# The last normalisation of the node block moved from the node stage into the first two graph layers

## The chip, the cores and the metric

The kernel runs on one core of a Trainium2 chip. The metric is the device time of one execution in microseconds (us). The engines of the core are named as in the profile: PE (TensorE, matmuls), DVE (VectorE), ACT (ScalarE), POOL (GpSimd) and SP (SyncE, which here only issues DMAs). Each engine works through its own instruction stream in order; semaphores tie the streams together, and DMA queues move data between DRAM and the on-chip memory (SBUF). Matmul results land in PSUM.

## The reference

A node table `x` of 50000 rows by 128 goes through four graph blocks, each followed by a residual add and a layer normalisation over the 128 columns. There are 25000 edges, so most nodes receive no edge.

```python
x = _layernorm(x + _L0_gnn_ref(x, ...))   # attention over 4 heads, gelu, norm, + x
x = _layernorm(x + _L1_gnn_ref(x, ...))   # three graph layers of width 128
x = _layernorm(x + _L2_gnn_ref(x, ...))   # attention over 8 heads
x = _layernorm(x + _L3_gnn_ref(x, ...))   # attention over 4 heads, edge gate
```

For a node without an incoming edge the last block comes down to its bias, so its output row is

```python
out = _layernorm(x3 + L3_gnn_bias)        # x3: the row after the third block
```

The kernel computes this row for all nodes and later overwrites the rows of nodes that have edges.

## The kernel before

The program is a list of stages with a barrier of all engines between them (`all_meet`). Three of them matter here.

**The node stage** (lines 400 to 829) treats every node as if it had no edges. It takes the 50176 padded rows in 49 chunks of 1024 rows, a chunk lying on the 128 partitions with 8 rows each (`wide`). It is a software pipeline written out by hand: in iteration `t` every engine does one piece for each of several chunks at different depths, and the order of the statements is the order on the engine. Six normalisations, LNA to LNF, belong to one chunk. DVE takes the statistics of each (`stats`, four BATCH_NORM_STATS2 of 256 columns), then once per iteration computes the inverse roots of all six together in ten short dependent instructions on a 128x48 block (lines 722 to 775, ending in `scaled`), and ACT applies scale and shift (`apply`, line 596, eight ACTIVATE of 128x128). After `scaled`, DVE goes on with the pieces of the chunks, ACT starts its own row of pieces, and PE works between them. SP stores each finished tile. LNF is the last: at lines 801 to 810 DVE waits for `x3` of chunk t-7, adds `bias3` into `hf_b` and takes its statistics; ACT applies LNF to `hf_b` one iteration later (lines 686 to 689); SP stores it to `out` (line 457). The rows before LNF, `x3_b`, are stored to a DRAM table (`tables[4]`) as well (line 452). Beside all that POOL gathers rows of the edges' ends by indirect DMA and writes an index map. The stage has 58 iterations.

**The graph layers** (lines 1502 to 1669) are one stage per layer, three in all, over the edges' rows in 49 chunks of 512. In iteration `t`: SP loads `own` (the chunk's own rows) and stores `xw` of chunk t-4, in this order and in one in-order stream, each store waiting for ACT. POOL gathers the source rows `gs` by four indirect DMAs a chunk, up to six chunks ahead. PE transposes `gs` and `own` and multiplies chunk t-2 by the next weights. DVE adds the bias to `own` (line 1630, four instructions), runs the segment scan (line 1635) and adds both (line 1642, `u`). ACT applies relu (line 1593, `hT`) and scales the product (line 1601, `xw`). The third layer has in addition a residual, statistics, square root and normalisation of its own (lines 1608, 1615, 1643 to 1668).

**The last stage** scatters the rows of the nodes with edges over `out` by indirect DMA (line 1789).

Of the kernel before, what the change touches and what calls it, by code (L numbers as in the profile page):

```python
# [47 lines left out]
def build(nc, x, src, dst, ea32, ea64, ew, w, out):  # L48
# [352 lines left out]
    with ExitStack() as tmp:  # L401
# [5 lines left out]
        z_b = ring("z_b", 2, (8, CH))  # L407
        x_in, t_b, x1_b, x2_b, hf_b = ring("x_in", 3), ring("t_b", 2), ring("x1_b", 3), ring("x2_b", 3), ring("hf_b", 3)
        xw_b = [ring(f"xw{k}_b", 2) for k in range(3)]
# [4 lines left out]

        raw = ring("raw", 2, (P, 6, 4, 6))
        rs, nm = ring("rs", 2, (P, 6, 8)), ring("nm", 2, (P, 6, 8))
        big, half_y, hx, wx = (ring(n, 1, (P, 48))[0] for n in ("big", "half_y", "hx", "wx"))
        shifted = tmp.enter_context(nc.sbuf_tensor("shifted", [P, 48], I32))
        LNA, LNB, LNC, LND, LNE, LNF = range(6)
        T_XT, T_H, T_G, T_A, T_B, T_C, T_D = ps[:, 0, :], ps[:, 1, :], (ps[:, 2, :], ps[:, 3, :]), ps[:, 4, :], ps[:, 5, :], ps[:, 6, :], ps[:, 7, :]  # L420

        def live(c):
            return 0 <= c < N_CH
# [11 lines left out]
        with nc.Block() as block:  # L435
            @block.sync
            def _(sp):
# [3 lines left out]

                for t in range(-1, N_CH + 8):
                    c = t + 1
# [9 lines left out]
                    if live(t - 3):  # L453
                        store(tables[0], xw_b[0], "xw0_out", 2, t - 3, "xw0", 2 * (t - 2))
                        store(tables[1], xw_b[1], "xw1_out", 2, t - 3, "xw1", 2 * (t - 2))
                    if live(t - 8):
                        store(out, hf_b, "out", 3, t - 8, "f_out", 2 * (t - 7))
                    if live(t - 3):
# [15 lines left out]
                for name, slots in (("x2_out", 3), ("x3_out", 2), ("xw0_out", 2), ("xw1_out", 2), ("xw2_out", 2), ("out", 3)):  # L474
                    for c in range(N_CH - slots, N_CH):
                        landed(sp, name, slots, c)
# [115 lines left out]
            def _(act):  # L592
# [14 lines left out]

                for t in range(N_CH + 9):
                    f, m = live(t), live(t - 3)
# [71 lines left out]
                    if edge(t):  # L681
# [3 lines left out]
                        nc.scalar.copy(xdT[t % 2][:], T_H).then_inc(S("xdT"), 1)  # L685
                    if live(t - 8):
                        q = t - 8
                        for h in range(2):
                            apply(LNF, hf_b[q % 3], lambda k: hf_b[q % 3][:, k * D:(k + 1) * D], r, b, h, "f_out")
                    if m:  # L690
# [4 lines left out]
            def _(v):  # L695
# [14 lines left out]
                v.wait_ge(S("raw"), 2)  # L710
                for t in range(N_CH + 9):
                    of = raw[(t - 1) % 2].rearrange("p n k (r s) -> p (n k r) s", r=2)
# [3 lines left out]
                    cw, cv, cw2 = t - 1, t - 4, t - 6  # L716
                    for name, back in (("a_st", 1), ("b_st", 2), ("c_st", 5), ("d_st", 6), ("e_st", 7), ("f_st", 8)):
                        if live(t - back):
                            v.wait_ge(S(name), 4 * (t - back + 1))
# [43 lines left out]
                    if live(t - 4):  # L763
                        v.wait_ge(S("b_out"), 2 * (t - 3))
                    if live(t - 10):
                        v.wait_ge(S("f_out"), 2 * (t - 9))
                    v.wait_ge(S("batch"), n0 + 9)
# [29 lines left out]
                    if live(t - 5):  # L797
# [4 lines left out]
                        stats(LND, t, pairs(hd_b[q % 2]), 0, 4, "d_st")  # L802
                    if live(t - 7):
                        q = t - 7
                        v.wait_ge(S("x3"), 2 * (q + 1))
                        if q >= 3:
                            landed(v, "out", 3, q - 3)
                        V.tensor_tensor(wide_rows(hf_b[q % 3][:]), wide_rows(x3_b[q % 2][:]), row_of_all(bias3), ALU.add).then_inc(S("hf"), 1)
                        v.wait_ge(S("hf"), q + 1)
                        stats(LNF, t, pairs(hf_b[q % 3]), 0, 4, "f_st")  # L810
                    if live(t):
# [690 lines left out]
    for layer in range(3):  # L1502
        last_layer = layer == 2
        new_phase()
        with ExitStack() as tmp:
# [9 lines left out]
            def live(c):  # L1515
                return 0 <= c < G_CH

            def edge_rows(table, c, base=NT):
                return table[base + c * CH:base + (c + 1) * CH, :].rearrange("(p j) f -> p (j f)", p=P)
# [8 lines left out]
            with nc.Block() as block:  # L1528
                @block.sync
                def _(sp):  # L1530
                    for t in range(G_CH + 8):
                        if live(t):
                            if t >= 4:
                                sp.wait_ge(S("own_ps"), t - 3)
                            sp.dma_start(own[t % 4][:], edge_rows(tables[layer], t)).then_inc(S(f"own_in{t % 4}"), 16)
                        if last_layer and live(t):
                            if t >= 8:
                                sp.wait_ge(S("v"), t - 7)
                            sp.dma_start(x1_e[t % 8][:], edge_rows(x1_slots, t, 0)).then_inc(S(f"x1_in{t % 8}"), 16)
                        c = t - (7 if last_layer else 4)  # L1540
                        if live(c):
                            sp.wait_ge(S("x2" if last_layer else "xw"), c + 1)
                            of = x2_e if last_layer else xw
                            sp.dma_start(edge_rows(tables[layer + 1], c), of[c % 3][:]).then_inc(S(f"stored{c % 3}"), 16)
                    for c in range(G_CH - 3, G_CH):
                        landed(sp, "stored", 3, c)

                @block.gpsimd
# [37 lines left out]
                def _(act):  # L1586
                    for t in range(G_CH + 8):
# [7 lines left out]
                        if live(c) and not last_layer:  # L1595
                            act.wait_ge(S("xw_ps"), c + 1)
                            if c >= 3:
                                landed(act, "stored", 3, c - 3)
                            for j in range(SUB):
                                k = c * SUB + j  # L1600
                                last = nc.scalar.activation(xw[c % 3][:, j * D:(j + 1) * D], T_W[c % 2][:, j * D:(j + 1) * D], ACT.Copy,  # L1601
                                                            scale=inv4[:, k:k + 1])
                            last.then_inc(S("xw"), 1)
                        c = t - 4
                        if live(c) and last_layer:
# [14 lines left out]
                def _(v):  # L1620
# [3 lines left out]
                    for t in range(G_CH + 7):  # L1624
# [12 lines left out]
                        if live(c):  # L1637
                            v.wait_ge(S("own_ps"), c + 1)
                            v.wait_ge(S("agg"), c + 1)
                            if c >= 2:  # L1640
                                v.wait_ge(S("hT"), c - 1)
                            V.tensor_tensor(rows4(u[c % 2][:]), agg[c % 3].rearrange("f (p j) -> f j p", j=SUB), rows4(T_O[c % 2]), ALU.add).then_inc(S("with_self"), 1)  # L1642
                        q = t - 4
                        if live(q) and last_layer:
# [467 lines left out]
```

## Time and profile before

| | us |
|---|---|
| median of 3 runs | 4333.93 |
| lowest and highest | 4331.24 and 4335.06 |
| the profiled execution, its own time | 4329.79 |
| its span in the profile | 4328.1 |

The granted clock of TensorE was 0.74 over the span. The stages show in the profile's slices: the node stage fills the first third (to 1435 us), a stage on the edges follows (to 1956), the three graph layers lie between 1956 and 2775, and two attention stages make up the rest. Over the span PE was busy 68%, DVE 80%, ACT 58% and POOL 58%. A busy share over the whole span says little here, since the stages have different limits; each has to be read by itself. A duration in a row is that of one instruction or of a run of like ones; "idle before" is the time for which the engine stood still ahead of it, with what ended it.

### The profile page before, as it was taken

Reading aid. Unit: us, or ns where it says so; the run is one execution under the profiler, and the core shown is the slowest. Engines: PE = TensorE matmul, PEld = TensorE weight load, DVE = VectorE, ACT = ScalarE, POOL = GpSimd, SP = SyncE. Lnnn points to the kernel's source line nnn. Section 1 sums busy time; section 2 is a strip of 40 time slices with the busy share of each in tenths; the row PEclk is TensorE's granted clock in tenths of the full one; section 3 lists DMA queues with packets and bytes.
Section 4 is the critical chain, followed back from the end, with each engine's and each line's share of the span. In section 5 each row is a group of like instructions: output and inputs, shape, how many; then the busy total and the mean of one; then the engine's idle time right before and its main releaser. Section 6 shows DMA issues by size and latency. Waiting matters only on the chain. (4 is left out here: it accounts for less than half of the span.)

```text
span 4328.1 us, 48774 instructions
## 1 busy us (share of the span) xinstructions
PE 2921.5 (68%) x12128; PEld 1943.4 (45%) x12128; DVE 3475.1 (80%) x8069; ACT 2494.4 (58%) x5486; POOL 2522.2 (58%) x2300
## 2 busy tenths in 40 slices
PE   5777767777673178874545545478888887677775
PEld 3544444454442034444545534345555554344443
DVE  5999999999998678875656679768777776788886
ACT  3777777777776256762323334446656565455554
POOL 6655555545450166626767767588666650766664
PEclk9998898888986578777767755577777776656555
DMA  4876666555553388854444456422222220333331
GB/s 114 178 186 186 185 190 187 186 190 187 187 181 132 103 246 255 252 165 124 152 128 151 152 164 198 154 62 72 66 68 64 67 62 28 106 88 87 92 95 49
DMA packets 383765, 599.12 MB, mean 138 GB/s; under 512 B 124231, under 2 KB 205296, under 8 KB 383486
## 3 DMA queue, kind: packets, MB, share of 16 engines
q1 hardware_dynamic: 313726, 482.99, 36.5%
q0 software_dynamic: 69760, 113.02, 10.5%
q8 instruction: 101, 1.65, 0.2%
q14 instruction: 178, 1.46, 0.1%
HBM read 312.45 MB, written 287.17 MB: 139 GB/s over the span
## 5 line engine op out<-in xcount | busy, mean ns | idle before, releaser
L1555 POOL DMA_INDIRECT gs_g<-table_xw,slot_idx x588 | 593.9, 1010 | 296.9 <-issue 263.7
L900 POOL DMA_INDIRECT gs_t<-table_x,slot_idx x392 | 421.5, 1075 | 300.8 <-issue 198.5
L495 POOL DMA_INDIRECT gs<-x,src_idx x200 | 224.2, 1121 | 441.1 <-DMA xd_rows<-gd 368.8
L368 PE MATMUL ps<-ident,gs_g 128*128 128x128 f32 x588 | 137.1, 377 | 363.2 <-DMA gs_g<-table_xw,slot_idx 363.2
L1593 ACT ACTIVATE hT_g<-u_g 128x512 f32<-128x512 f32 x147 | 92.5, 629 | 497.7 <-DVE u_g L1642 497.7
L1272 POOL DMA_INDIRECT slot_idx<-node_map,src_idx x200 | 242.8, 1214 | 190.9 <-DMA slot_idx<-node_map,src_idx 94.6
L1635 DVE TENSOR_TENSOR_SCAN agg_g<-same_seg,agg_g,ps 128x512 f32<-128x512 uint8 x147 | 188.0, 1279 | 173.9 <-PE ps L368 173.6
L483 POOL DMA_INDIRECT node_map<-slot_no,end_idx x200 | 278.8, 1394 | 60.9 <-issue 60.3
L1789 POOL DMA_INDIRECT out<-x_t,end_idx x196 | 205.6, 1049 | 169.6 <-ACT x_t L339 116.9
L368 PEld LDWEIGHTS ps<-ident,gs_g 128*128 128x128 f32 x588 | 90.0, 190 | 402.6 <-issue 352.0
L495 POOL DMA_INDIRECT gd<-x,dst_idx x200 | 215.4, 1077 | 60.9 <-issue 60.0
L1848 PE MATMUL ps<-xsT_t,Wv 128*128 128x512 f32 x196 | 152.3, 870 | 133.0 <-DVE msg_t L953 132.8
L900 POOL DMA_INDIRECT own_t<-table_x,own_idx x196 | 200.3, 1022 | 59.7 <-issue 59.7
L1630 DVE SCALAR_TENSOR_TENSOR own_g<-bs_row,root,own_g 128x128 f32<-128x128 f32 x588 | 167.2, 346 | 48.7 <-DMA own_g<-table_xw 48.2
L628 ACT ACTIVATE h1T<-ps,h_bias 128x512 f32<-128x512 f32 x49 | 33.7, 687 | 268.7 <-DVE nm L775 267.9
L1940 ACT COPY xsT_t<-ps 128x512 f32<-128x512 f32 x49 | 28.7, 585 | 250.3 <-PE ps L368 250.3
L596 ACT ACTIVATE x_b<-v_b,nm,rs 128x128 f32<-128x128 f32 x392 | 156.6, 497 | 19.4 <-DVE nm L775 19.4
L596 ACT ACTIVATE x_b<-s_b,nm,rs 128x128 f32<-128x128 f32 x392 | 156.8, 497 | 17.1 <-DVE nm L775 17.1
L596 ACT ACTIVATE hf_b<-hf_b,nm,rs 128x128 f32<-128x128 f32 x392 | 157.5, 514 | 2.4 <-DVE nm L775 2.4
L596 ACT ACTIVATE x_b<-t_b,nm,rs 128x128 f32<-128x128 f32 x392 | 157.4, 510 | 0.0
L374 PE MATMUL ps<-WS,hT_g 128*128 128x128 f32 x784 | 152.9, 362 | 5.5 <-ACT xw_g L1601 5.5
L1913 ACT COPY xsT_t<-ps 128x512 f32<-128x512 f32 x98 | 56.4, 576 | 171.8 <-PE ps L368 171.8
(362 smaller groups left out, 10071.3 us busy)
## 6 DMA issues: line engine op xcount, KB each, us to landing
table_xw<-xw_b SPq DMA_DIRECT2D x147, 512.0 KB, 5.4
table_x<-x_b SPq DMA_DIRECT2D x98, 512.0 KB, 2.7
own_g<-table_xw SPq DMA_DIRECT2D x147, 256.0 KB, 3.7
x_in<-x SPq DMA_DIRECT2D x49, 512.0 KB
out<-hf_b SPq DMA_DIRECT2D x49, 512.0 KB, 2.9
table_xw<-xw_g SPq DMA_DIRECT2D x98, 256.0 KB
pen_t<-pen_row SPq DMA_DIRECT2D x98, 256.0 KB, 4.1
xd_rows<-gd SPq DMA_DIRECT2D x50, 256.0 KB, 5.6
```

The lines of the kernel that those rows point to most:

```text
L368: last = nc.tensor.transpose(to[0:width, j * P:(j + 1) * P], t[:, j * width:(j + 1) * width], ident[:])
L374: last = nc.tensor.matmul(to[:, j * D:(j + 1) * D], tT[:, j * P:(j + 1) * P], W[:], start=True, stop=bias_row is None)
L483: pool.indirect_dma_start(out=node_map, out_offset=bass.IndirectOffsetOnAxis(ap=end_idx[:, t:t + 1], axis=0), in_=slot_no[:, t:t + 1], in_ ...
L495: pool.indirect_dma_start(out=to[k % 3][:, j * D:(j + 1) * D], out_offset=None, in_=x, in_offset=bass.IndirectOffsetOnAxis(ap=of[:, n:n + ...
L596: last = nc.scalar.activation(to[:, k * D:(k + 1) * D], of(k), ACT.Identity, scale=r[:, n, k:k + 1], bias=b[:, n, k:k + 1])
L900: pool.indirect_dma_start(out=self.B[L % RING][g][:, t * D:(t + 1) * D], out_offset=None, in_=table, in_offset=bass.IndirectOffsetOnAxis(a ...
L1272: pool.indirect_dma_start(out=slot_idx[:, t:t + 1], out_offset=None, in_=node_map, in_offset=bass.IndirectOffsetOnAxis(ap=src_idx[:, t:t + ...
L1555: pool.indirect_dma_start(out=gs[c % 6][:, j * D:(j + 1) * D], out_offset=None, in_=tables[layer], in_offset=bass.IndirectOffsetOnAxis(ap= ...
L1630: V.scalar_tensor_tensor(out=blk, in0=bs_row[layer][:], scalar=root4[:, k:k + 1], in1=blk, op0=ALU.mult, op1=ALU.add).then_inc(S("own_bias ...
L1635: V.tensor_tensor_scan(agg[t % 3][:], same_seg[:, t * CH:(t + 1) * CH], T_X[t % 2], agg[(t - 1) % 3][:, CH - 1:CH], ALU.mult, ALU.add).the ...
L1789: pool.indirect_dma_start(out=out, out_offset=bass.IndirectOffsetOnAxis(ap=end_idx[:, k:k + 1], axis=0), in_=B[L % RING]["x4"][:, t * D:(t ...
L1848: nc.tensor.matmul(K[3], (Wv if kind == 2 else Wv3)[:], B[L % RING]["xsT"][:], start=True, stop=True).then_inc(S("v_ps"), 1)
```

## The change

LNF leaves the node stage. The batch there shrinks from 48 to 40 columns, the stage from 58 to 57 iterations, and SP no longer stores to `out`. The three tiles `hf_b` go.

The same work on the same 49 wide chunks is now done in the first two graph layers, 25 chunks in the first and 24 in the second, one in every second iteration. SP loads the rows of `tables[4]` back from DRAM (`y`, 512 KB), DVE adds the bias and takes the statistics three iterations later, ACT takes the square root (a Sqrt activation in place of the node stage's batch on DVE), DVE the reciprocal and the shift, ACT applies them in place six iterations after the load, and SP stores the tile to `out` after eight.

```diff
-        raw = ring("raw", 2, (P, 6, 4, 6))
+        raw = ring("raw", 2, (P, 5, 4, 6))
...
-                    if live(t - 8):
-                        store(out, hf_b, "out", 3, t - 8, "f_out", 2 * (t - 7))
...
-                for t in range(N_CH + 9):
+                for t in range(N_CH + 8):
...
-                    if live(t - 8):
-                        q = t - 8
-                        for h in range(2):
-                            apply(LNF, hf_b[q % 3], lambda k: hf_b[q % 3][:, k * D:(k + 1) * D], r, b, h, "f_out")
...
-                    if live(t - 10):
-                        v.wait_ge(S("f_out"), 2 * (t - 9))
+                    if live(t - 9):
+                        v.wait_ge(S("x3"), 2 * (t - 8))
...
-                    if live(t - 7):
-                        q = t - 7
-                        v.wait_ge(S("x3"), 2 * (q + 1))
-                        if q >= 3:
-                            landed(v, "out", 3, q - 3)
-                        V.tensor_tensor(wide_rows(hf_b[q % 3][:]), wide_rows(x3_b[q % 2][:]), row_of_all(bias3), ALU.add).then_inc(S("hf"), 1)
-                        v.wait_ge(S("hf"), q + 1)
-                        stats(LNF, t, pairs(hf_b[q % 3]), 0, 4, "f_st")
...
+            y = [tmp.enter_context(nc.sbuf_tensor(f"y_g{layer}_{k}", [P, 2 * CH], F32)) for k in range(5)]
+            y_st, y_sd, y_rs, y_nm = (ring(n, 3, k) for n, k in (("y_st", 24), ("y_sd", 8), ("y_rs", 8), ("y_nm", 8)))
+            N_Y = (N_CH + 1 - layer) // 2 if layer < 2 else 0
+
+            def node_chunk(t):
+
+                return t // 2 if t % 2 == 0 and 0 <= t // 2 < N_Y else None
+
+            def of_all(k):
+                return (layer * ((N_CH + 1) // 2)) + k
...
+                        k = node_chunk(t)
+                        if k is not None:
+                            if k >= 5:
+                                landed(sp, "y_out", 5, k - 5)
+                            sp.dma_start(y[k % 5][:], wide(tables[4], of_all(k))).then_inc(S(f"y_in{k % 5}"), 16)
+                        k = node_chunk(t - 8)
+                        if k is not None:
+                            sp.wait_ge(S("y"), k + 1)
+                            sp.dma_start(wide(out, of_all(k)), y[k % 5][:]).then_inc(S(f"y_out{k % 5}"), 16)
...
+                        k = node_chunk(t - 4)
+                        if k is not None:
+                            act.wait_ge(S("y_st"), 4 * (k + 1))
+                            squares = y_st[k % 3].rearrange("p (j t) -> p j t", t=3)[:, :, 2]
+                            nc.scalar.activation(y_sd[k % 3][:], squares, ACT.Sqrt, bias=eps[:, 0:1], scale=1.0 / D).then_inc(S("y_sd"), 1)
+                        k = node_chunk(t - 6)
+                        if k is not None:
+                            act.wait_ge(S("y_nm"), k + 1)
+                            for j in range(2 * SUB):
+                                blk = y[k % 5][:, j * D:(j + 1) * D]
+                                last = nc.scalar.activation(blk, blk, ACT.Identity, scale=y_rs[k % 3][:, j:j + 1], bias=y_nm[k % 3][:, j:j + 1])
+                            last.then_inc(S("y"), 1)
...
+                        k = node_chunk(t - 3)
+                        if k is not None:
+                            landed(v, "y_in", 5, k)
+                            V.tensor_tensor(wide_rows(y[k % 5][:]), wide_rows(y[k % 5][:]), row_of_all(bias3), ALU.add).then_inc(S("y_bias"), 1)
+                            v.wait_ge(S("y_bias"), k + 1)
+                            if k >= 3:
+                                v.wait_ge(S("y_sd"), k - 2)
+                            for n in range(4):
+                                V.bn_stats(y_st[k % 3][:, 6 * n:6 * n + 6], row_pair(y[k % 5], n)).then_inc(S("y_st"), 1)
+                        k = node_chunk(t - 5)
+                        if k is not None:
+                            v.wait_ge(S("y_sd"), k + 1)
+                            if k >= 3:
+                                v.wait_ge(S("y"), k - 2)
+                            V.reciprocal(y_rs[k % 3][:], y_sd[k % 3][:]).then_inc(S("y_rs"), 1)
+                            v.wait_ge(S("y_rs"), k + 1)
+                            mean = y_st[k % 3].rearrange("p (j t) -> p j t", t=3)[:, :, 1]
+                            V.scalar_tensor_tensor(out=y_nm[k % 3][:], in0=mean, scalar=-1.0, in1=y_rs[k % 3][:],
+                                                   op0=ALU.mult, op1=ALU.mult).then_inc(S("y_nm"), 1)
```

DVE in one iteration of the node stage before (`hd_b` and `hf_b` are the inputs of LND and LNF, `s_b` that of LNE):

```order
L700 BN_STATS raw<-t_b 128x6 x4
L800 TENSOR_TENSOR hd_b<-x_b,bo 128x1024
L700 BN_STATS raw<-hd_b 128x6 x4
L808 TENSOR_TENSOR hf_b<-x_b,bias 128x1024
L700 BN_STATS raw<-hf_b 128x6 x4
L700 BN_STATS raw<-ps 128x6 x2
L818 SCALAR_TENSOR_TENSOR d_b<-hd_b,raw,gamma 128x128 x8
```

The same place in the changed kernel:

```order
L694 BN_STATS raw<-t_b 128x6 x4
L794 TENSOR_TENSOR hd_b<-x_b,bo 128x1024
L694 BN_STATS raw<-hd_b 128x6 x4
L694 BN_STATS raw<-ps 128x6 x2
L804 SCALAR_TENSOR_TENSOR d_b<-hd_b,raw,gamma 128x128 x8
```

Two entries, five instructions, are gone, and with them DVE's wait for `x3`.

DVE in two iterations of the first graph layer of the changed kernel (before, only the rows of `own`, `agg` and `u` stand there, over and over):

```order
L1650 SCALAR_TENSOR_TENSOR own_g_1<-bs_row,root,own_g_1 128x128 x4
L1655 SCALAR_TENSOR_TENSOR agg_g_1<-same_seg,agg_g_0,ps 128x512
L1662 TENSOR_TENSOR u_g_0<-agg_g_0,ps 128x512
L1666 TENSOR_TENSOR y_g_0<-y_g_0,bias 128x1024
L1671 BN_STATS y_st_g_2<-y_g_0 128x6 x4
L1677 RECIPROCAL y_rs_g_1<-y_sd_g_1 128x8
L1680 SCALAR_TENSOR_TENSOR y_nm_g_1<-y_st_g_1,y_rs_g_1 128x8
L1650 SCALAR_TENSOR_TENSOR own_g_2<-bs_row,root,own_g_2 128x128 x4
L1655 SCALAR_TENSOR_TENSOR agg_g_2<-same_seg,agg_g_1,ps 128x512
L1662 TENSOR_TENSOR u_g_1<-agg_g_1,ps 128x512
```

All seven new instructions of DVE lie in one of the two iterations, between `u` and the next `own`.

SP in two iterations of the same layer, changed kernel (before, a load of `own` and a store of `xw` alternate and nothing else stands there):

```order
L1532 DMA own_g_2<-table_xw 128x512
L1541 DMA y_g_1<-table_x 128x1024
L1545 DMA out<-y_g_2 128x1024
L1550 DMA table_xw<-xw_g_0 128x512
L1532 DMA own_g_3<-table_xw 128x512
L1550 DMA table_xw<-xw_g_1 128x512
L1532 DMA own_g_0<-table_xw 128x512
```

The load and the store of `y` both come between one load of `own` and the next store of `xw`, and the load of `own` behind that store stands behind both.

## Rows read from the trace of the kernel before

**Rows 1.** Busy time in stretches: us, PE, PEld, DVE, ACT, POOL, PEclk, DMA share, GB/s.
```profile
200.00:1300.00 1100.00, 791.51 (x3911) 532.42 (x3909) 1080.02 (x3056) 860.05 (x1996) 595.34 (x487) 0.89 0.61 186
1965.00:2220.00 255.00, 137.27 (x763) 127.11 (x763) 160.75 (x288) 75.87 (x227) 192.92 (x193) 0.75 0.47 143
2510.00:2760.00 250.00, 133.78 (x555) 105.63 (x556) 227.06 (x614) 109.75 (x252) 192.42 (x190) 0.52 0.62 190
```

**Rows 2.** Waits of DVE, 400 to 1200 us: us in total, times, longest.
```profile
DVE hf_b L808 <- ACT x_b L596: 5.2, 29, 0.2
```

**Rows 3.** Timeline of DVE in the node stage: start us, us, instruction, idle before.
```profile
1013.22 1.22 DVE L808 TENSOR_TENSOR hf_b<-x_b,bias 128x1024 f32<-128x1024 f32 x1 [0.17 <-ACT x_b L596]
1014.47 1.43 DVE L700 BATCH_NORM_STATS2 raw<-hf_b 128x6 f32<-128x256 f32 x4
...
1022.90 0.19 DVE L722 TENSOR_SCALAR big<-raw 128x48 f32<-128x48 f32 x1
...
1049.87 0.19 DVE L722 TENSOR_SCALAR big<-raw 128x48 f32<-128x48 f32 x1
```

**Rows 4.** Timeline of ACT in the same iteration.
```profile
1003.67 0.69 ACT L628 ACTIVATE h1T<-ps,h_bias 128x512 f32<-128x512 f32 x1 [5.88 <-DVE nm L775]
...
1005.39 0.59 ACT L602 COPY xT<-ps 128x512 f32<-128x512 f32 x1
...
1019.18 3.21 ACT L596 ACTIVATE hf_b<-hf_b,nm,rs 128x128 f32<-128x128 f32 x8
```

**Rows 5.** Timeline of PE in the same iteration.
```profile
1019.46 1.86 PE L529 MATMUL ps<-xsT,att_src 128*8 128x512 f32 x2 [3.22 <-ACT xdT L685]
...
1028.78 0.60 PE L368 MATMUL ps<-ident,x_in 128*128 128x128 f32 x4
```

**Rows 6.** Timeline of the node stage's end.
```profile
1412.50 1.22 DVE L808 TENSOR_TENSOR hf_b<-x_b,bias 128x1024 f32<-128x1024 f32 x1 [3.25 <-ACT x_b L596]
...
1426.75 0.32 SPq L440 DMA_DIRECT2D table_x<-x_b  x1
...
1439.50 0.33 SPq L1020 DMA_DIRECT2D cont<-nst_row  x1
```

**Rows 7.** Groups of the first graph layer, 1965 to 2220 us: busy us, mean ns, idle before.
```profile
L1555 POOL DMA_INDIRECT gs_g<-table_xw,slot_idx x193 | 193.9, 1005 | 58.8 <-issue 58.5 <-DMA gs_g<-table_xw,slot_idx 0.3
```

**Rows 8.** Timeline of the first graph layer.
```profile
2087.00 0.43 SPq L1535 DMA_DIRECT2D own_g<-table_xw  x1
...
2088.43 1.28 DVE L1635 TENSOR_TENSOR_SCAN agg_g<-same_seg,agg_g,ps 128x512 f32<-128x512 uint8 x1 [1.58 <-PE ps L368]
...
2089.62 1.05 DVE L1642 TENSOR_TENSOR u_g<-agg_g,ps 128x512 f32<-128x512 f32 x1
...
2090.70 0.63 ACT L1593 ACTIVATE hT_g<-u_g 128x512 f32<-128x512 f32 x1 [4.09 <-DVE u_g L1642]
2090.87 1.14 DVE L1630 SCALAR_TENSOR_TENSOR own_g<-bs_row,root,own_g 128x128 f32<-128x128 f32 x4 [0.20 <-DMA own_g<-table_xw]
...
2091.24 1.12 ACT L1601 ACTIVATE xw_g<-ps,inv 128x128 f32<-128x128 f32 x4
```

**Rows 9.** Timeline of DVE and POOL in the node stage.
```profile
632.88 1.21 DVE L800 TENSOR_TENSOR hd_b<-x_b,bo 128x1024 f32<-128x1024 f32 x1
632.90 2.06 POOL L495 DMA_INDIRECT gd<-x,dst_idx  x1 [0.30 <-issue]
...
1014.09 1.22 POOL L483 DMA_INDIRECT node_map<-slot_no,end_idx  x1 [0.30 <-issue]
```

**Rows 10.** DMA issues of the whole run: count, KB each, median us to landing.
```profile
table_xw<-xw_b SPq DMA_DIRECT2D x147, 512.0 KB, 5.4
table_x<-x_b SPq DMA_DIRECT2D x98, 512.0 KB, 2.7
own_g<-table_xw SPq DMA_DIRECT2D x147, 256.0 KB, 3.7
```

**Rows 11.** Timeline of the first graph layer's end.
```profile
2227.24 1.14 ACT L1601 ACTIVATE xw_g<-ps,inv 128x128 f32<-128x128 f32 x4 [0.69 <-PE ps L374]
...
2232.13 9.46 SPq L1535 DMA_DIRECT2D own_g<-table_xw  x5
```

**Rows 12.** Groups of ACT in the third graph layer, 2505 to 2770 us.
```profile
L1608 ACT ACT_TABLE_LOAD x1 | 1.3, 1283 | 0.0
```

More of the change, by code:

```diff
@@ L407, in build @@
         z_b = ring("z_b", 2, (8, CH))
-        x_in, t_b, x1_b, x2_b, hf_b = ring("x_in", 3), ring("t_b", 2), ring("x1_b", 3), ring("x2_b", 3), ring("hf_b", 3)
+        x_in, t_b, x1_b, x2_b = ring("x_in", 3), ring("t_b", 2), ring("x1_b", 3), ring("x2_b", 3)
         xw_b = [ring(f"xw{k}_b", 2) for k in range(3)]
@@ L412, in build @@
         xT, gT, x1T, h1T, h2T = (ring(n, 2, (P, CH)) for n in ("xT", "gT", "x1T", "h1T", "h2T"))
-        raw = ring("raw", 2, (P, 6, 4, 6))
[L416 to L419, printed above, removed]
+        raw = ring("raw", 2, (P, 5, 4, 6))
+        rs, nm = ring("rs", 2, (P, 5, 8)), ring("nm", 2, (P, 5, 8))
+        big, half_y, hx, wx = (ring(n, 1, (P, 40))[0] for n in ("big", "half_y", "hx", "wx"))
+        shifted = tmp.enter_context(nc.sbuf_tensor("shifted", [P, 40], I32))
+        LNA, LNB, LNC, LND, LNE = range(5)
         T_XT, T_H, T_G, T_A, T_B, T_C, T_D = ps[:, 0, :], ps[:, 1, :], (ps[:, 2, :], ps[:, 3, :]), ps[:, 4, :], ps[:, 5, :], ps[:, 6, :], ps[:, 7, :]
@@ L440, in store @@
                     sp.dma_start(wide(table, c), rows[c % slots][:]).then_inc(S(f"{name}{c % slots}"), 16)
-                for t in range(-1, N_CH + 8):
+                for t in range(-1, N_CH + 7):
                     c = t + 1
@@ L473, in _ @@
                         landed(sp, name, slots, k)
-                for name, slots in (("x2_out", 3), ("x3_out", 2), ("xw0_out", 2), ("xw1_out", 2), ("xw2_out", 2), ("out", 3)):
+                for name, slots in (("x2_out", 3), ("x3_out", 2), ("xw0_out", 2), ("xw1_out", 2), ("xw2_out", 2)):
                     for c in range(N_CH - slots, N_CH):
@@ L710, in _ @@
                 v.wait_ge(S("raw"), 2)
-                for t in range(N_CH + 9):
+                for t in range(N_CH + 8):
                     of = raw[(t - 1) % 2].rearrange("p n k (r s) -> p (n k r) s", r=2)
@@ L716, in _ @@
                     cw, cv, cw2 = t - 1, t - 4, t - 6
-                    for name, back in (("a_st", 1), ("b_st", 2), ("c_st", 5), ("d_st", 6), ("e_st", 7), ("f_st", 8)):
+                    for name, back in (("a_st", 1), ("b_st", 2), ("c_st", 5), ("d_st", 6), ("e_st", 7)):
                         if live(t - back):
@@ L1546, in _ @@
                         landed(sp, "stored", 3, c)
+                    for k in range(max(0, N_Y - 5), N_Y):
+                        landed(sp, "y_out", 5, k)
                 @block.gpsimd
```

## The prediction

> **What bounds the kernel now.** I read the busy time by stage first, then the waits of the busiest engine in each, then the timelines to see what a freed microsecond runs into.
>
> In the node stage DVE is busy 1080 of 1100 us [rows 1], and from 400 to 1200 us all it waits for is ACT ahead of `hf_b`, 0.18 us each time [rows 2]. So DVE sets the pace there, one iteration in 1049.87 - 1022.90 = 26.97 us [rows 3]. ACT stands still for 5.88 us of it, until DVE's last batch instruction releases it [rows 4].
>
> In the first graph layer DVE is busy 63% and ACT 30% [rows 1]. POOL issues gathers without a break: 1.005 us busy and 58.8/193 = 0.305 us between two [rows 7], 1.31 us each, 5.24 us for the four of a chunk, 10.5 us for a pair of chunks. Its idle time is "issue", so nothing holds it back, and 49 chunks make the stage. DVE waits for PE, and PE's gathered rows come at POOL's pace [rows 8]. So POOL sets the pace. The third layer is a trial of the change in advance: DVE is busy there 227 of 250 us and POOL 192, the same as in the first layer [rows 1]. 0.91 x 5.24 = 4.8 us of DVE work a chunk still hide beside the gathers.
>
> **What the node stage gives back.** Five DVE instructions go: 0.17 us of waiting, 1.25 us from the start of the bias add to the statistics, 1.43 us of statistics [rows 3], together 2.85 us. The ten batch instructions lose 8 of 48 columns; an estimate from the 0.19 us for 48 columns [rows 3] is at most 0.03 us each and, since most of such a short instruction is fixed cost, I take 0.08 us for all ten. That makes 2.93 us an iteration, for 48 of the 49 chunks: 140.6 us. One iteration of the drain waits 3.25 instead of 0.17 us [rows 6]: 3.1 us more. The stage's end: the last `x3` store is issued at 1426.75 and the next stage starts at 1439.50 [rows 6]. At the end of a graph layer, 3.75 us pass from the last ACT instruction's end (2228.38) to the next stage's first DMA [rows 11]; with that the next stage starts at about 1430.4, 9.1 us earlier. Sum: 152.8, say 153 us.
>
> This holds if DVE still sets the pace at 24.04 us an iteration. ACT's row of pieces takes 26.97 - 5.88 = 21.1 us and loses its eight applies, some 3.1 us; it then fits with 6 us to spare. PE is what comes next. It waits for ACT's `xdT` until 1019.46, 15.8 us after ACT's row starts, and ends its own row at 1028.78 + 0.60 = 1029.38, 25.7 us after [rows 4, 5]. Nothing ahead of `xdT` is removed, so PE ends at 25.7 us again while the next row of ACT starts at 24.04: PE begins each row 1.7 us late. The first piece of ACT that needs that last PE result is the copy of `xT`, 1.72 us into the row [rows 4]: it just fits. So I take the whole 2.93, and for the range that up to 0.6 us an iteration is lost there (28 us). A loss below nothing I exclude, since no piece is added to this stage. The node stage's removed store (512 KB an iteration, at a DMA share of 0.61) only lightens the queues.
>
> **What the graph layers pay.** Per pair of chunks DVE gets, all in one iteration, the add and the statistics (1.25 + 1.43 us, [rows 3]) and two instructions on 8 columns, about 0.4 us by the 0.19 us of the 48-column one. The old part is 1.19 from scan to `u`, 1.05 for `u` and 1.14 for `own` [rows 8], 3.38 us a chunk. The pair comes to 6.76 + 3.08 = 9.84 us against 10.5 us of POOL: hidden, by little. ACT gets eight applies (3.2 us, [rows 4]) and a root of about 0.3 us, beside two times 0.63 + 1.12 [rows 8]: 7.0 us, hidden. A table load for the root occurs once in the third layer, which mixes root, relu and scale [rows 12], so I count one of 1.3 us.
>
> Three things are not hidden.
>
> *POOL is held up by the wide add.* A POOL DMA instruction issued at 632.90, 0.02 us after a DVE add of 128x1024 from two SBUF tiles, took 2.06 us instead of 1.0 and ended 0.8 us after the add; another, issued 0.87 us into such an add, took 1.22 [rows 9, 3]. The new `y` add has the same form, and in the layers POOL has no slack. With a gather started every 1.31 us and an add of 1.22 us, one gather starts within nearly every add and waits 0 to 1.06 us, on average (uniform phase) about 0.45 us. Over 49 adds: 22 us, bounds 0 and 52.
>
> The Trainium skill (SBUF — State Buffer, "Who interferes with whom") says that a DVE instruction with two SBUF inputs contends with a GpSimd instruction that reads SBUF, but that `tensor_tensor` did not stall descriptor generation in its own probe. By the second half these 22 us would be nothing; the trace disagrees, with 2.06 us in the row named, and I go by the trace.
>
> *The loads of `own` queue behind the `out` stores.* SP waits for ACT's `xw`, stores it, and loads `own` two chunks ahead; the load of 2087.00 lands just before 2090.87, where DVE waits 0.20 us for it [rows 8]. So it is nearly late already. Follow one pair, from the scan of the iteration with `y` (0): DVE reaches the next scan at 1.19 + 1.05 + 3.08 + 1.14 = 6.46 us, `u` ends 2.24 later, then ACT: relu 0.63, `xw` 1.12, root 0.3, applies 3.2, at 13.95; relu and `xw` of the next chunk to 15.7; SP issues `own` at 16.1; it lands after L; the bias on `own` takes 1.14; the scan that is two pairs on. So two pairs last at least 17.2 + L, a pair (17.2 + L)/2. With L = 3.7 [rows 10] that is 10.45, just hidden. But the `out` store of 512 KB is issued right after the applies, 2 us ahead of that load. Two 512 KB stores issued together land after 5.4 us and one alone after 2.7 [rows 10], so 512 KB ahead costs up to 2.7 us, less the 2 us that it is ahead, and the `y` load shares the engines: L between 3.7 and 6.4, I take 4.9. The pair is then 11.05 us.
>
> The Trainium skill (DMA: Bandwidth & Descriptors, "Queues, rings and completion order") says that the copies of one issuing engine go to the same rings and start in order; by that rule the load stands fully behind the store, L = 6.4, and a pair is 11.8 us. The 5.4 against 2.7 us of the trace agree with it for stores issued together.
>
> These two overlap rather than add: a POOL that is held up (10.95) gives the load of `own` its time. I take 11.05, 0.55 us over the pair's 10.5: 49 x 0.55 = 27 us. The bounds are 0 (both hidden) and 1.3 us a pair, 64 us.
>
> *The drain of the layers.* The last `y` chunk of the first layer passes through ACT at iteration 54, behind the last `xw` (done at 2228.38, [rows 11]): a root (0.3) and two sets of applies (6.4), and its 512 KB store: 7 us later than now. In the second layer, with one chunk fewer, one set: 3.5 us. With a longer store landing by a little: 10 us together, bounds 6 and 16.
>
> The gathers' descriptors share the engines with 1 MB more a pair, and the DMA share should go from 0.47 to about 0.75; the third layer ran at 0.62 with POOL's pace unchanged [rows 1]. POOL is up to six chunks ahead, 31 us, so a longer landing of a gather costs nothing in pace. POOL has no new entry.
>
> **Sum.** The profiled execution took 4329.8 us: 4329.8 - 153 + 27 + 10 = 4213.8. The median is 4.1 us above that execution, so 4218 us.
>
> **Rivals.**
> (a) *The layers hide it all.* For: the third layer. Against: rows 9, where a wide add stops POOL. Cost 10 instead of 37: 4191 us.
> (b) *The layers become bound by SP's chain through ACT.* With L = 6.4 or more, or applies that arrive later than counted, a pair takes 11.8 to 12.7 us: +64 to +108 us, 4255 to 4300. For: the load of `own` has only 0.2 us to lose now. Against: the store has 2 us head start on it.
> (c) *PE takes over in the node stage.* PE is late by 1.7 us and the copy of `xT` has no slack; a lower granted clock (0.89 there, 0.52 in the third layer, [rows 1]) would lengthen its 9.9 us between `xdT` and the row's end. If half of the gain goes: 4218 + 70 = 4288 us.
> (d) *Slower than before.* One mechanism: the loads of `own` behind 1 MB of `y` traffic. It outweighs the node stage's gain once a pair costs (153 - 10)/49 = 2.9 us more than 10.5, a pair of 13.4 us, that is L above 9.6 us. The median load of `own` lands after 3.7 us [rows 10], so it would need the queue to hold more than two 512 KB transfers all the time. Its time would be 4340 us and up.
> That the change doesn't do what it says would mean DVE keeps 27 us an iteration; with the instructions gone from a 98% busy engine I give it nothing of its own.
>
> **How the numbers follow.** Forecast (4200 to 4250) 0.60; (a) 0.14; (b) 0.14; (c) 0.08; (d) 0.03; the rest between. A measurement of this kernel can tell 0.2% from no change, some 9 us. Every case but (d), and the far end of (c), is faster: 0.95 faster, 0.02 same, 0.03 slower. The range takes in (a) and the near part of (b): 4186 to 4272.
>
> **What would show it.** The node stage ends at about 1280 to 1290 us with an iteration of 24.0 us, and DVE waits for nothing in it; a new wait for PE of some tenths would be (c). In the first two layers a pair of chunks takes 11.0 us; single gathers of 1.2 to 2.0 us beside the `y` add prove the first mechanism, and a DVE wait at the first `own` bias after an `out` store, for a DMA that lands after more than 4.5 us, the second. The third layer and all stages behind it keep their length. I am wrong if the layers grow by more than 40 us each or the node stage shrinks by less than 125.

## The result, and the profile after

| | before | changed |
|---|---|---|
| median | 4334.5 us | 4227.6 us |
| lowest and highest of 4 | 4331.2, 4343.2 | 4224.9, 4232.3 |
| ratio of the runs | | 0.9749, 95% interval 0.9735 to 0.9764 |
| span of the profiled execution | 4328.1 us | 4230.3 us |

Forecast were 4218 us and 4186 to 4272. The change is faster by 107 us. What happened stage by stage is read from where each stage's first DMA starts, in the profiles of before, of the changed kernel and of five of the experiments told below:

| us | before | changed | node part alone | PSUM bias | spread | spread + PSUM | own early |
|---|---|---|---|---|---|---|---|
| node stage, from 0 to the next stage's start | 1439.5 | 1285.5 | 1286.3 | 1286.7 | 1286.4 | 1288.1 | 1285.9 |
| stage on the edges | 519.9 | 524.0 | 518.7 | 517.2 | 522.7 | 520.6 | 521.8 |
| first graph layer | 272.7 | 297.7 | 272.6 | 290.5 | 284.6 | 278.8 | 300.2 |
| second graph layer | 272.8 | 294.3 | 272.9 | 284.9 | 281.3 | 273.7 | 297.4 |
| third layer and all behind it | 1823.2 | 1828.8 | 1828.9 | 1826.8 | 1833.8 | 1837.7 | 1832.6 |

The node stage gives 154.0 us. The first two layers take back 25.0 and 21.5 us. The last row and the one of the edge stage differ by some us also between kernels whose code there is the same, up and down; that is the profile's own scatter. 154.0 - 46.5 = 107.5 us is close to the difference of the medians, 106.9; in the two profiled spans, 97.8 us apart, 4 and 6 us of scatter lie on top.

The waits of DVE in the node stage of the changed kernel from 200 to 1150 us (us in total, times, longest), where before it waited for ACT [rows 2]:

```profile
DVE h_b L719 <- ACT xw_b L686: 0.9, 3, 0.4
```

One iteration of DVE there, from its timeline; before it was 26.97 us [rows 3]:

```profile
904.52 0.19 DVE L716 TENSOR_SCALAR big<-raw 128x40 f32<-128x40 f32 x1
...
928.54 0.19 DVE L716 TENSOR_SCALAR big<-raw 128x40 f32<-128x40 f32 x1
```

It is 24.02 us, with 0.9 us of waiting in some forty iterations: DVE still sets the pace. PE stands idle there, ahead of the scores, as it did before [rows 5]; its timeline:

```profile
927.97 1.87 PE L527 MATMUL ps<-xsT,att_src 128*8 128x512 f32 x2 [3.23 <-ACT xdT L683]
```

Busy time in stretches of the changed kernel, the columns as in [rows 1], node stage and first layer:

```profile
200.00:1150.00 950.00, 728.59 (x3787) 495.47 (x3788) 938.07 (x2762) 721.23 (x1618) 606.62 (x476) 0.91 0.69 188
1815.00:2090.00 275.00, 155.93 (x776) 138.54 (x776) 229.60 (x458) 148.94 (x433) 203.71 (x193) 0.69 0.67 220
```

In the first layer DVE is now busy 83%, ACT 54%, and the DMA engines carry 220 instead of 143 GB/s. The granted clock of TensorE rose in the node stage, from 0.89 to 0.91, and fell in the first layer, from 0.75 to 0.69; PE's busy time over that whole layer went from 141.7 to 158.0 us.

POOL's gathers in the first and in the second layer of the changed kernel (busy us, mean ns of one, idle before); before, the first layer's 193 had a mean of 1005 ns [rows 7]:

```profile
L1563 POOL DMA_INDIRECT gs_g<-table_xw,slot_idx x196 | 207.6, 1059 | 144.3 <-issue 143.4 <-PE ps L368 0.6 <-DMA gs_g<-table_xw,slot_idx 0.3
```
```profile
L1563 POOL DMA_INDIRECT gs_g<-table_xw,slot_idx x196 | 209.2, 1068 | 90.1 <-issue 59.1 <-POOLq L83 30.7 <-DMA gs_g<-table_xw,slot_idx 0.3
```

The same 196 gathers took 196.9 and 197.3 us before: 10.7 and 11.9 us more, 22.6 together. They wait for PE and for DMA only 0.9 us in the first layer and 0.3 in the second, so POOL was hardly ever held by its consumers. Where the time sits in a single gather, from the timeline of the changed kernel:

```profile
1889.84 1.22 DVE L1666 TENSOR_TENSOR y_g<-y_g,bias 128x1024 f32<-128x1024 f32 x1
1889.94 1.99 POOL L1563 DMA_INDIRECT gs_g<-table_xw,slot_idx  x1 [0.30 <-issue]
```

A gather that starts 0.10 us into the add ends 0.87 us after it, as in [rows 9]. The same holds over both layers: 44 gathers start inside one of the 49 adds, and each of the 42 that start 0.08 to 1.08 us into it ends 0.86 to 0.89 us after it. The later a gather starts in the add, the less it waits; together these gathers wait 23 us.

The other half of the growth lies behind the last gather. "POOLq L83" in the second row is how long POOL stood at the barrier between the two layers: 30.7 us, before 16.4. ACT in that stretch of the first layer:

```profile
2086.69 3.19 ACT L1622 ACTIVATE y_g<-y_g,y_nm_g,y_rs_g 128x128 f32<-128x128 f32 x8
...
2092.48 3.22 ACT L1622 ACTIVATE y_g<-y_g,y_nm_g,y_rs_g 128x128 f32<-128x128 f32 x8
...
2096.74 6.31 ACT L1622 ACTIVATE y_g<-y_g,y_nm_g,y_rs_g 128x128 f32<-128x128 f32 x16
```

Four sets of applies, 12.7 us, are still to come when POOL is done (2077.2). The first of them starts 9.5 us later, after a wait of ACT for DVE's `u`; from 2084.96 to 2103.05 ACT then works without a break, and the next layer's first DMA starts at 2107.21. Before, ACT's last instruction ended at 2228.38, 12 us after POOL, and the next layer began 3.75 us later [rows 11].

### The profile page after: what moved, and what is told of

It reads as the page before. It is cut to its first block and busy times, and to the rows that moved or that the text cites. A ratio compares the mean times of both kernels' runs of the same rounds, so it can differ in the third digit from the quotient of the medians.

```text
span 4230.3 us, 49000 instructions
## 1 busy us (share of the span) xinstructions
PE 2899.9 (69%) x12128; PEld 1933.6 (46%) x12128; DVE 3478.3 (82%) x8156; ACT 2509.0 (59%) x5535; POOL 2568.4 (61%) x2300
## 5 line engine op out<-in xcount | busy, mean ns | idle before, releaser
L1563 POOL DMA_INDIRECT gs_g<-table_xw,slot_idx x588 | 616.8, 1049 | 319.5 <-issue 261.9
L493 POOL DMA_INDIRECT gs<-x,src_idx x200 | 223.9, 1119 | 292.2 <-DMA xd_rows<-gd 211.0
L1258 POOL DMA_INDIRECT slot_idx<-node_map,src_idx x200 | 242.1, 1211 | 196.9 <-DMA slot_idx<-node_map,src_idx 103.6
L481 POOL DMA_INDIRECT node_map<-slot_no,end_idx x200 | 302.6, 1513 | 60.9 <-issue 60.0
L374 PE MATMUL ps<-WS,hT_g 128*128 128x128 f32 x784 | 163.1, 378 | 9.6 <-ACT xw_g L1609 9.3
L368 PE MATMUL ps<-ident,own_g 128*128 128x128 f32 x588 | 146.5, 398 | 29.0 <-DVE own_g L1650 28.0
L374 PEld LDWEIGHTS ps<-WS,hT_g 128*128 128x128 f32 x784 | 154.9, 293 | 11.8 <-issue 11.2
```

What stands on the lines that cost most here:

```text
L368: last = nc.tensor.transpose(to[0:width, j * P:(j + 1) * P], t[:, j * width:(j + 1) * width], ident[:])
L374: last = nc.tensor.matmul(to[:, j * D:(j + 1) * D], tT[:, j * P:(j + 1) * P], W[:], start=True, stop=bias_row is None)
L481: pool.indirect_dma_start(out=node_map, out_offset=bass.IndirectOffsetOnAxis(ap=end_idx[:, t:t + 1], axis=0), in_=slot_no[:, t:t + 1], in_ ...
L493: pool.indirect_dma_start(out=to[k % 3][:, j * D:(j + 1) * D], out_offset=None, in_=x, in_offset=bass.IndirectOffsetOnAxis(ap=of[:, n:n + ...
L1258: pool.indirect_dma_start(out=slot_idx[:, t:t + 1], out_offset=None, in_=node_map, in_offset=bass.IndirectOffsetOnAxis(ap=src_idx[:, t:t + ...
L1563: pool.indirect_dma_start(out=gs[c % 6][:, j * D:(j + 1) * D], out_offset=None, in_=tables[layer], in_offset=bass.IndirectOffsetOnAxis(ap= ...
```

## The experiments

Each kernel is timed against the kernel before on its own chip; not all ran on the same one. The median of the kernel before lay between 4333.7 and 4335.2 us in all groups of runs, so medians of different groups can be compared to within a few us.

**The node part alone.** The changed kernel with `N_Y = 0`, which leaves the moved normalisation out.

```diff
-            N_Y = (N_CH + 1 - layer) // 2 if layer < 2 else 0
+            N_Y = 0
```

> The node stage of the changed kernel, and nothing of the moved normalisation in the graph layers: the rows of nodes without edges are left out of the output. If the node stage's gain (154 us in the profiles) is all of its own making and the 10 us by which the untouched stages differ are chance, 4334 - 154 = 4180 us, and the graph layers take 272.8 us each as before. If those 10 us belong to the changed node stage (another state of the queues or of the clock behind it), the edge stage stays at 524 us instead of 520 and the time is 4184 to 4190.

Measured: 4182.6 us, ratio 0.9647 (0.9618 to 0.9676). The layers take 272.6 and 272.9 us, the edge stage 518.7. Expected were 4180 us. So the node stage's gain is its own, the edge stage's 4 us in the changed kernel are scatter, and the moved work costs 4227.6 - 4182.6 = 45 us, by the profiles all of it in the two layers.

**The add alone**, in the kernel before:

```diff
+                        if not last_layer and t % 2 and 3 <= t < 3 + 2 * (25 - layer):
+                            v.wait_ge(S("probe"), (t - 3) // 2)
+                            V.tensor_tensor(wide_rows(probe[1][:]), wide_rows(probe[0][:]), row_of_all(bias3), ALU.add).then_inc(S("probe"), 1)
```

> The kernel before, with one DVE add of 128x1024 from two SBUF tiles in every second iteration of the first two graph layers (25 and 24), its result unused, no DMA, no ACT work. Theory (the wide add holds up POOL's gathers): the gathers' mean rises from 1.005 to about 1.06 us, the two layers' gather phases by 10 to 12 us each, the time to about 4356. Rival (POOL is held up by the DMA traffic of the moved rows, not by the add): mean stays at 1.005 and the time at 4334.

**The same add with its bias in PSUM** (`bias3` copied once a layer to a PSUM bank that the layers leave free). The copy and the two probe buffers are in both kernels, which differ in this line alone:

```diff
-... wide_rows(probe[0][:]), row_of_all(bias3), ALU.add)
+... wide_rows(probe[0][:]), row_of_all(ps[:, 6, 0:D]), ALU.add)
```

> As the kernel with the add alone, but the bias is read from a PSUM bank, so that the add has one SBUF input. Theory (two SBUF inputs are what locks POOL out): the gathers' mean is back at 1.005 us and the layers at 272.8 us, time 4334. Rival (any wide DVE instruction beside a gather costs the same, or DVE's fuller row does): the same 1.06 us and 4356 as with the SBUF bias.

Measured: 4342.6 and 4344.2 us, one run each, where 4356 and 4334 were expected; with single runs of this scatter the totals tell nothing, and the second profile has 6 us more in the untouched edge stage. The gathers of the first layer tell them apart, first with the add from SBUF, then with the one from PSUM:

```profile
L1556 POOL DMA_INDIRECT gs_g<-table_xw,slot_idx x196 | 202.3, 1032 | 134.1 <-issue 133.8 <-DMA gs_g<-table_xw,slot_idx 0.3
```
```profile
L1556 POOL DMA_INDIRECT gs_g<-table_xw,slot_idx x196 | 196.7, 1004 | 154.3 <-issue 153.7 <-DMA gs_g<-table_xw,slot_idx 0.6
```

With the SBUF add the gathers are 5.4 and (second layer) 6.5 us longer than before, without any DMA or ACT work beside it; with the PSUM add they are as before (196.7 and 197.4). The kind of operand does it, neither DVE's load nor DMA traffic. The size is half of what was expected: 0.24 us an add here, 0.46 in the changed kernel. The two traces show why. As in the changed kernel, 44 gathers start inside an add, and a held one ends just as long after it, here 0.87 us:

```profile
2381.83 1.21 DVE L1648 TENSOR_TENSOR probe_g<-probe_g,bias 128x1024 f32<-128x1024 f32 x1
...
2382.18 1.73 POOL L1556 DMA_INDIRECT gs_g<-table_xw,slot_idx  x1 [0.30 <-issue]
```

But this is the longest one in these two layers. No gather starts in the first 0.35 us of an add here, while in the changed kernel the starts lie all over it, so these gathers wait 14 us together and not 23. With the PSUM operand 44 gathers start inside an add too, and all take 0.99 to 1.01 us.

**The changed kernel with its bias in PSUM.** The same edit at `y`'s add.

> The changed kernel with the bias of the moved normalisation read from PSUM. Theory (POOL's hold-up is all of the 22.6 us by which the two gather phases grew): mean back to about 1.01 us, both gather phases at 256 to 258 us, 4228 - 22 = 4206 us. Rival (SP's chain, an own load behind an out store, is as near as predicted): the pair of chunks falls only to what that chain allows, 10.8 us and more, gathers wait for PE, and at most 5 us are won: 4223.

Measured: 4207.7 us, ratio 0.9715 (0.9691 to 0.9740), by the medians 20 us less than the changed kernel, by the ratios 15; the two layers of the profile are 16.6 us shorter. The gathers, first layer, and what PE and DVE wait for there:

```profile
L1563 POOL DMA_INDIRECT gs_g<-table_xw,slot_idx x196 | 198.0, 1010 | 141.6 <-issue 140.4 <-PE ps L368 0.9 <-DMA gs_g<-table_xw,slot_idx 0.3
```
```profile
PE ps L368 <- DVE own_g L1651: 62.1, 34, 5.6
DVE own_g L1651 <- DMA own_g<-table_xw: 22.2, 21, 1.9
```

All of POOL's 22.6 us but 0.7 are gone, and the time from a layer's first to its last gather is 257.4 and 256.3 us, as expected. What was not expected is the other side: the layers fell only to 290.5 and 284.9 us, and POOL stands 33.0 us at the barrier between the first two. PE waits 62 us for `own` in the first layer, in the changed kernel 10; the experiments with the loads of `own` below show that this wait by itself says little. The consumers have fallen further behind: the last chunk's scan in the first layer starts 7.5 us after its last gather's end, in the changed kernel 5.5 and before 3.1, and five and four sets of applies start behind a layer's last gather instead of four and three. POOL runs up to six chunks ahead, so this shows only in the drain. It is a lag and not a slower pace. Two scans, twenty chunks apart:

```profile
1857.21 1.28 DVE L1656 TENSOR_TENSOR_SCAN agg_g<-same_seg,agg_g,ps 128x512 f32<-128x512 uint8 x1 [1.55 <-PE ps L368]
...
1963.46 1.27 DVE L1656 TENSOR_TENSOR_SCAN agg_g<-same_seg,agg_g,ps 128x512 f32<-128x512 uint8 x1
```

That is 10.6 us for a pair of chunks.

**The chunks dealt out as 22, 21 and 6**, the six in the third layer:

```diff
-            N_Y = (N_CH + 1 - layer) // 2 if layer < 2 else 0
+            N_Y, EVERY = (22, 21, 6)[layer], (2, 2, 8)[layer]
...
-                return t // 2 if t % 2 == 0 and 0 <= t // 2 < N_Y else None
+                return t // EVERY if t % EVERY == 0 and 0 <= t // EVERY < N_Y else None
...
-                return (layer * ((N_CH + 1) // 2)) + k
+                return (0, 22, 43)[layer] + k
```

> The changed kernel with the 49 moved chunks dealt out as 22, 21 and 6 (the six in the third layer, one in every eighth iteration), so that the last one enters six iterations before a layer's last gathers. Theory (the other half of the layers' growth, 14.3 and 9.5 us between the last gather and the next stage, is ACT working off four sets of applies that were still open): both drains back to 17 to 19 us, the hold-up of POOL unchanged at 0.23 us a chunk and now in part in the third layer, time 4228 - 20 = 4208 us. Rival (the third layer, with DVE busy 91%, has no room): it grows by 10 us or more and the time stays at 4220 or above.

Measured: 4212.7 us, ratio 0.9715 (0.9694 to 0.9737), 15 us less (4208 were expected; the four runs lie between 4200 and 4220). POOL's stand at the barriers behind the first two layers is 19.3 and 16.1 us, as expected, and the two layers are 13.1 and 13.0 us shorter than in the changed kernel. The third layer, read to its own end (286.4 us in the changed kernel), is 294.4 us: 8 us for six chunks, of which 6 lie in the gathers. TensorE's clock does not make the drain: it is 0.67 in the second layer here, as low as in the changed kernel, and POOL's stand behind that layer is 16.1 us, as before. Of ACT's four sets of applies behind the last gather one is left:

```profile
2081.99 3.19 ACT L1622 ACTIVATE y_g<-y_g,y_nm_g,y_rs_g 128x128 f32<-128x128 f32 x8
```

**The DMAs of `y` issued by ACT** instead of SP, the store right behind the applies:

```diff
-                            sp.wait_ge(S("y"), k + 1)
-                            sp.dma_start(wide(out, of_all(k)), y[k % 5][:]).then_inc(S(f"y_out{k % 5}"), 16)
+                            act.wait_ge(S("y"), k + 1)
+                            act.dma_start(wide(out, of_all(k)), y[k % 5][:]).then_inc(S(f"y_out{k % 5}"), 16)
```

> The changed kernel with the loads and the out stores of y issued by ACT instead of SP, so that no load of own stands behind them in SP's stream. Theory (the loads of own did not set the pace, POOL did): gather phases and time unchanged within 5 us, 4228, or a few us more for the issuing on ACT. Rival (the predicted chain of SP holds part of the growth): DVE's waits for own go, and the gather phases shrink by 5 us or more each, 4215.

**Each load of `own` one chunk earlier**, into a ring of five buffers instead of four, with `y` as in the changed kernel:

```diff
-                            if t >= 4:
-                                sp.wait_ge(S("own_ps"), t - 3)
+                            if t >= 5:
+                                sp.wait_ge(S("own_ps"), t - 4)
...
-                        c = t - (7 if last_layer else 4)
+                        c = t - (7 if last_layer else 5)
```

> The changed kernel, nothing moved, but SP stores xw five iterations back instead of four and own has five buffers, so that each load of own is issued one chunk (5 us) earlier and no longer stands right behind ACT's applies and the out store. Theory (in the changed kernel POOL is the pace and own's loads are not): gather phases as before (267 and 269 us), time 4228, DVE's waits for own gone. Rival (the predicted chain takes part in the growth): gather phases 5 us shorter each and 4215.

Measured: 4236.3 us (0.9772, 0.9757 to 0.9787) and 4236.4 us (0.9766, 0.9747 to 0.9785). Neither is faster than the changed kernel; both are some 9 us slower, where 4228 were expected. DVE's wait for the loads of `own` in the first layer, with the loads earlier:

```profile
DVE own_g L1650 <- DMA own_g<-table_xw: 3.7, 5, 2.2
```

In the changed kernel this wait was 14.0 us, less than the 24.6 us of before; it went to 3.7, and the layer did not become shorter (300.2 against 297.7 us). The gather phases kept their length, 267.8 and 268.8 us against 267.0 and 268.7. In the version with ACT's queue the last gather of the first layer ended 267 us after the first, as in the changed kernel, but both layers became longer (301.3 us each) and PE waited 70 us for DVE's `own`. With the loads earlier it waited 67 us, in the changed kernel 10, so this wait grows whether POOL is held up or not and does not measure what a layer costs. That ACT's issuing and waiting holds up its relu is a possible reason for the longer layers with ACT's queue; it was not tested by itself. The loads behind the stores did not set the pace.

**Both remedies, and what is left.** Spread and PSUM bias together, the same with the loads of `own` earlier, with the applies split four and four over two iterations (SP stores one iteration later, six buffers), and with `y`'s DMAs on ACT:

> The 22, 21, 6 dealing and the bias from PSUM together. Theory (hold-up and drain are the two halves and add): 4228 - 20 - 20 = 4188 us, within 8 us of the node stage's part alone (4182.6). Rival (with POOL released DVE's backlog grows and eats the drain's gain): 4200.

> The same with the DMAs of y issued by ACT. If the loads of own limit once POOL is released, this is faster than the version on SP by 3 us or more; if not, equal or slower by ACT's issuing, 4188 to 4195.

> Bias from PSUM, chunks dealt 22, 21, 6, and the loads of own issued one chunk earlier. With POOL released PE waited 67 us for DVE's own bias in the first layer, and DVE 24 us for the loads behind it. If the chain over SP is what holds DVE back there, both waits go, the drain falls from 21.3 to 16.5 us, and the time from 4193 to 4185. If DVE's own fullness in the iterations with y holds it back, DVE's wait goes and PE's stays, and the time is 4193.

> Bias from PSUM, chunks dealt 22, 21, 6, and ACT's eight applies split over two iterations (four and four), loads of own as in the changed kernel. If ACT's block of 3.2 us is the link of the chain that counts, xw and with it own come 1.6 us earlier and the time goes from 4193 to 4187; if not, it stays at 4193 within 3 us.

> Both: own loaded one chunk earlier and the applies split. Hoped for: 4183 us, as fast as the changed kernel without any moved work in the layers (4182.6). If the third layer's six chunks and its full DVE are what is left, 4190.

| | median | ratio to before (95%) |
|---|---|---|
| spread + PSUM bias | 4193.2 | 0.9674 (0.9661 to 0.9687) |
| with ACT's queue | 4211.1 | 0.9715 (0.9700 to 0.9730) |
| with `own` earlier | 4195.4 | 0.9679 (0.9664 to 0.9693) |
| with split applies | 4195.6 | 0.9681 (0.9666 to 0.9696) |
| with both of these | 4194.2 | 0.9675 (0.9661 to 0.9689) |

The first is the fastest complete version, 34 us below the changed kernel and 11 above the node part alone; those with the loads earlier, the applies split, or both, cannot be told from it. Expected were 4188 us if the two remedies add and 4200 if the lag eats the drain's gain, and 4193 lies between. ACT's queue costs 18 us more, beyond the 4188 to 4195 expected for it. The waits moved as hoped and the time, hoped for at 4183 to 4187 us, did not: with `own` earlier DVE's wait for its loads in the first layer went from 24.5 to 7.5 us and PE's for DVE only from 67.5 to 62.6. In the profiles 6 us of what remains lie in the first layer, 1 in the second and some 6 in the third (292.2 us against 286.4). A full DVE in the iterations with `y` fits this; it was not shown. Nor was it shown whether the lower granted clock of TensorE (0.68 in the first layer, before 0.75) takes part in the lag.

## Why the prediction was right

- *The node stage, 153 us.* Measured 154.0, with 24.02 us an iteration against 24.04. The last `x3` store is issued 146.1 us earlier (1280.62 after 1426.75), forecast were 143.7; the stage's end gives 7.9 us, forecast 9.1. That DVE would go on setting the pace, and PE's small slack would do, holds: 0.9 us of DVE's waits in 950 us. Rival (c) did not come.
- *POOL and the wide add, 22 us.* The two gather phases grew by 22.6 us, and reading the bias from PSUM took all but 0.7 of it away. The mean wait of 0.45 us was worked out from starts that lie evenly over the add, and in the changed kernel they do: 0.46. That they would was luck, since the add by itself met later starts and gave 0.24. Rival (a) is refuted with it. Of the two statements of the Trainium skill (SBUF — State Buffer, "Who interferes with whom") that the prediction sets side by side, the trace agrees with the first for these gathers, which read their indices from SBUF, and not with the second, on the page's own probe: a `tensor_tensor` of two SBUF inputs did hold them up, by up to 1.0 us, and one with a PSUM input did not.
- *`own` behind the `out` stores, 5 us more, and up to 64.* This step failed. Its chain was to set a pair at 11.05 us. POOL's hold-up, which the prediction put at 10.95 a pair, was the pace: 10.9 and 11.0 us (267.0 and 268.7 us for 49 chunks). So the pair came out as forecast, but by the smaller of the two terms. The load itself was sized nearly right: where DVE waited for a load issued behind an `out` store, in 23 cases in the two layers, its work on it started 4.5 us after the issue in the median, where L = 4.9 was taken. (In 17 more it had not to wait. The 4.2 us that the profile gives for `own`, 3.7 before, cover only 24 of the 147 loads, and the nearest of them to an `out` store was issued 5.4 us behind it.) By the formula 4.5 us would still make a pair 10.85. But with the bias in PSUM the scans come every 10.6 us, and with the loads one chunk earlier the gather phases did not become shorter. So the chain has slack that the sum did not count; which of its links was counted too long stays open. With it falls what rivals (b) and (d) rest on. The consumers do fall behind POOL, but by a lag that is paid once at the barrier, and of that lag the loads are not the cause that counts.
- *The drain, 10 us.* The mechanism was right and the size wrong: 14.3 and 9.5 us, 23.8 together. I counted the sets of applies behind the last `xw` in ACT's stream, two and one. But POOL is ahead of ACT, and what counts is all that ACT has open when the last gather is done: four sets in the first layer, three in the second.
- *The sum.* The layers cost 46.5 us where 37 were forecast: the pace term 4 too high, the drain 14 too low, so that a part of the one miss hides in the other. The profiled execution is the slowest of the changed kernel's four, in line with its 10 us more in stages that nobody touched.
- *The third layer as a trial in advance* was read for POOL's pace alone. It has a DVE just as full but no wide add with two SBUF inputs, and in the kernel before its gathers take 259 us from the first to the last, against 256 in the first layer. It also showed the drain in advance. Its last gather ends at 2764.79 and the next stage's first DMA starts at 2790.43, 25.6 us later, where the first layer needs 15.7; ACT's last instruction there ends 22 us after the last gather, against 12 in the first layer:

```profile
2783.74 3.17 ACT L1615 ACTIVATE x_e_g<-v_b_g,nm_g,rs_g 128x128 f32<-128x128 f32 x8
```

## What to carry to other kernels

Work moved beside an engine that sets the pace is not free because the other engines have room: look whether its instructions hold up that engine, as here a long DVE instruction with two SBUF inputs held up POOL's gathers, and try such an instruction with a PSUM operand. Let moved work end some iterations before the stage does: what is still open when the pacing engine is done is paid at the barrier, and taking it out earlier was worth 15 us here for three lines. And read a trial in advance for its drain too, not only for its pace.

## What the runs showed of the hardware

- A 128x1024 float32 add takes as long with its broadcast operand in PSUM (1.21 us in the changed kernel with the PSUM bias) as with both in SBUF (1.22).
- A gather that starts within such an add with two SBUF inputs ends 0.86 to 0.89 us after it (42 cases in the changed kernel, 39 with the add alone), against 1.00 us from start to end without an add beside it. The one gather that started 0.01 us into an add was not held.
- Short instructions hold POOL as well, by the length of their row. In the first layer before, the 45 gathers that start within a row of four 128x128 (`own`, 1.14 us) take 1.03 us in the mean and at most 1.13. In the node stage before, from 200 to 1300 us, POOL's DMA instructions that start within a row of eight with two SBUF inputs (`d_b`, line 818) take 1.95 us in the mean (68 of them), within a row of four with two SBUF inputs (`t_b`, line 792) 1.20 (72), and within a row of four with one of its inputs in PSUM (`a_b`, line 788) 1.01 (62). The longest, an index-map write, starts at the end of one row of eight and is held through the next:

```profile
263.02 3.40 POOL L483 DMA_INDIRECT node_map<-slot_no,end_idx  x1 [0.31 <-issue]
263.34 2.18 DVE L822 SCALAR_TENSOR_TENSOR s_b<-d_b,rs,s_b 128x128 f32<-128x128 f32 x8
```

- The edge stage, with the same code, took between 517.2 and 525.6 us from one profile to the next, so that a term of a few us is to be read from its own rows and not from the total.
